# One product of ones for the exponentials of key tiles 0 and 1, summed by GpSimd, and a rewritten order of a group

## The reference, cut to what matters

```python
x = x + L0_attn(layernorm(x)); x = x + L0_ffn(layernorm(x))
x = x + L1_attn(layernorm(x)); x = x + L1_ffn(layernorm(x))
# both attentions: 2 batches x 1024 positions, 32 query heads and 8 key/value heads of 32
q, k, v = rope(x @ wq), rope(x @ wk), x @ wv
scores = einsum('bqhd,bkhd->bhqk', q, k) / sqrt(32) + causal_mask
attn = softmax(scores, axis=-1)                # exp(scores - rowmax) / sum over keys
out = einsum('bhqk,bkhd->bqhd', attn, v) @ wo
```

## Time and profile before

| | |
|---|---|
| median of 3 runs | 2916.91 us (2914.6 to 2921.62) |
| profiled execution | 2913.83 us, span of its instructions 2912.1 us |
| busy PE / DVE / ACT / POOL | 90% / 62% / 38% / 39% |
| mean granted TensorE clock | 0.952 of 2.4 GHz |
| PE in 118 to 497 us (groups of layer 0, batch 0) | 351.56 of 379 us busy |
| PE in 164 to 211 us (one of these groups) | idle 0.8 us |

### The profile page before, as it was taken

The page is one execution under the profiler, slowest core; times in us unless marked ns, Lnnn a source line. Parts: engine busy times, 40 slices in busy tenths (PEclk is TensorE's granted clock), DMA queues, the critical chain, the costliest instruction groups (busy, mean ns, idle before and its releaser), DMA issues. The chain is left out here.

```text
span 2912.1 us, 50930 instructions
## 1 busy us (share of the span) xinstructions
PE 2608.1 (90%) x15312; PEld 1828.1 (63%) x15312; DVE 1797.7 (62%) x4437; ACT 1095.2 (38%) x2381; POOL 1123.9 (39%) x801
## 2 busy tenths in 40 slices
PE   7999997999998799791969999979999987997999
PEld 6665653765654588681857565537656544876887
DVE  5677775667775433588756777765677753215543
ACT  2345454145555211470622454541354553002000
POOL 7456553546564100000054656545466642002110
PEclk9999998999999999896979999989999998998999
DMA  4323222422321421000244232213232314434111
GB/s 158 110 78 93 84 61 66 140 84 80 98 77 38 168 72 58 1 1 0 98 151 124 74 103 67 82 66 120 80 104 77 93 40 152 147 109 149 71 60 44
DMA packets 121086, 253.05 MB, mean 87 GB/s; under 512 B 12720, under 2 KB 39728, under 8 KB 120880
## 3 DMA queue, kind: packets, MB, share of 16 engines
q1 hardware_dynamic: 120912, 251.03, 27.0%
HBM read 166.57 MB, written 84.41 MB: 86 GB/s over the span
## 5 line engine op out<-in xcount | busy, mean ns | idle before, releaser
L617 ACT ACTIVATE a_prob<-a_pst 128x512 f32<-128x512 f32 (+3 forms) x1536 | 660.6, 493 | 560.4 <-PE a_pst L898 555.1
L710 DVE CUSTOM_DVE_ANT_0 a_psh<-a_psh,a_edge 128x128 f32<-128x128 f32 (+3 forms) x1024 | 479.7, 516 | 193.6 <-PE a_psh L851 172.6
L898 PE MATMUL a_pst<-a_qst,a_kst 128*128 128x512 f32 (+2 forms) x1536 | 487.9, 372 | 24.0 <-DMA a_qst<-rowmax 19.0
L851 PE MATMUL a_psh<-a_kst,a_qst 127*128 127x512 f32 (+3 forms) x1536 | 484.2, 363 | 16.2 <-DVE a_mx L710 6.1
L517 POOL TENSOR_TENSOR a_prob<-a_prob 128x2048 f32<-128x2048 f32 (+1 forms) x96 | 405.6, 4226 | 239.7 <-PE a_ppv L914 239.7
L851 PEld LDWEIGHTS a_psh<-a_kst,a_qst 127*128 127x128 f32 x1536 | 272.0, 189 | 229.8 <-DVE a_mx L713 92.7
L713 DVE TENSOR_REDUCE a_mx<-a_psh 128x1 f32<-128x512 f32 x512 | 329.1, 685 | 124.7 <-PE a_psh L851 123.7
L898 PEld LDWEIGHTS a_pst<-a_qst,a_kst 128*128 128x128 f32 x1536 | 287.5, 194 | 167.1 <-ACT a_prob L617 104.3
L914 PE MATMUL a_ppv<-a_prob,a_vg 128*32 128x512 f32 (+3 forms) x3072 | 319.8, 503 | 0.0
L502 POOL TENSOR_SCALAR_AFFINE_SELECT a_prob<-a_prob 128x512 f32<-128x512 f32 x256 | 161.8, 639 | 192.3 <-ACT a_prob L617 192.2
L927 PE MATMUL a_pden<-a_prob,a_ones 128*32 128x512 f32 (+3 forms) x2304 | 222.5, 479 | 14.1 <-POOL a_prob L517 14.1
(11 more groups left out here) (231 smaller groups left out, 4208.3 us busy)
## 6 DMA issues: line engine op xcount, KB each, us to landing
a_qst<-q SPq DMA_DIRECT2D x192, 256.0 KB, 4.5
a_wraw<-in_wqkv SPq DMA_DIRECT2D x52, 512.0 KB, 4.3
q<-a_stg_hi SPq DMA_DIRECT2D x64, 256.0 KB, 2.1
q<-a_stg_lo SPq DMA_DIRECT2D x64, 256.0 KB, 2.4
a_kst<-kT SPq DMA_DIRECT2D x96, 128.0 KB, 2.5
oT<-a_oT SPq DMA_DIRECT2D x32, 256.0 KB, 2.4
oT<-a_vT SPq DMA_DIRECT2D x32, 256.0 KB, 2.9
h_oraw<-oT SPq DMA_DIRECT2D x16, 512.0 KB, 4.0
```

The source lines that it names most:

```text
L617: act.activation(prob[k % len(prob)][:, h, off:], pst[:, (k * GH + h) % 3, off:], ACT.Exp, scale=scale).then_inc(s["exp_done"], 1)
L710: part = dve.tensor_tensor_reduce(scores, scores, edge[:, BANK - n:], 1.0, 2 * MASKED, ALU.add, ALU.max, mx_hq[kc][:, h, qt:qt + 1])
L851: mm = pe.matmul(psh[:, at, i * n:(i + 1) * n], qst[par][0:P - 1, h, qt * P:(qt + 1) * P], kst[par][0:P - 1, kc * BANK:kc * BANK + n], sta ...
L898: pe.matmul(pst[:, (k * GH + h) % 3, off:], kst[par][:, ki * P:(ki + 1) * P], qst[par][:, h, qc * BANK + off:(qc + 1) * BANK], start=True, ...
```

## The change

The new text of `ORDER`, nothing else. `SUM:0+1` and `D:0+1` take the place of `D:0` and `D:1`: POOL adds the 384 columns of each head of unit 1 onto unit 0, and one product of 512 columns per head gives the denominators of both. Around it most words of the group stand in another place.

```diff
     P:0.0 P:0.1
-    ST:0.0 WL ST:0.1 ST:0.2 S P:0.2 ST:0.3 P:0.3
-    ST:1.0 ST:1.1 P:0.4 ST:1.2 S HI:1 ST:1.3 P:0.5
-    ST:2.0 ST:2.1 P:0.6 LO:1 S P:0.7 ST:2.2 S ST:2.3
-    ST:3.0 V:0 D:0 S S ST:3.1 ST:3.2 S ST:3.3 V:1
-    ST:4.0 ST:4.1 RS:1 ST:4.2 HI:0 S S D:1 ST:4.3 LO:0
-    ST:5.0 S ST:5.1 S V:2 V:3 D:2 D:3 S ST:5.2 S ST:5.3 S V:4 S
...
-    ST:11.0 S ST:11.1 ST:11.2 P:1.0 P:1.1 ST:11.3 S P:1.2 S D:8+9 WS V:10 V:11 RK D:10 D:11 MT P:1.3
-      NORM:0 P:1.4 P:1.5 P:1.6 P:1.7 NORM:1 VG
+    ST:0.0 WL ST:0.1 ST:0.2 P:0.2 P:0.3 ST:0.3
+    ST:1.0 S ST:1.1 P:0.4 ST:1.2 S ST:1.3 HI:1 LO:1 P:0.5
+    ST:2.0 V:0 S ST:2.1 RS:1 S SUM:0+1 ST:2.2 ST:2.3 P:0.6 P:0.7
+    ST:3.0 ST:3.1 S ST:3.2 V:1 ST:3.3 S S S D:0+1
+    ST:4.0 S ST:4.1 ST:4.2 S S ST:4.3 V:2 HI:0 D:2 S
+    ST:5.0 ST:5.1 S V:3 S ST:5.2 LO:0 S ST:5.3
...
+    ST:11.0 ST:11.1 P:1.1 ST:11.2 ST:11.3 WS S S V:10 D:8+9 V:11 D:10 D:11 P:1.2 MT NORM:0 P:1.3 RK P:1.4
+      VG P:1.5 NORM:1 P:1.6 P:1.7
```

More of the change, by code:

```diff
@@ L78 @@
     P:0.0 P:0.1
-    ST:0.0 WL ST:0.1 ST:0.2 S P:0.2 ST:0.3 P:0.3
-    ST:1.0 ST:1.1 P:0.4 ST:1.2 S HI:1 ST:1.3 P:0.5
-    ST:2.0 ST:2.1 P:0.6 LO:1 S P:0.7 ST:2.2 S ST:2.3
-    ST:3.0 V:0 D:0 S S ST:3.1 ST:3.2 S ST:3.3 V:1
-    ST:4.0 ST:4.1 RS:1 ST:4.2 HI:0 S S D:1 ST:4.3 LO:0
-    ST:5.0 S ST:5.1 S V:2 V:3 D:2 D:3 S ST:5.2 S ST:5.3 S V:4 S
[L85 to L89, removed]
-    ST:11.0 S ST:11.1 ST:11.2 P:1.0 P:1.1 ST:11.3 S P:1.2 S D:8+9 WS V:10 V:11 RK D:10 D:11 MT P:1.3
-      NORM:0 P:1.4 P:1.5 P:1.6 P:1.7 NORM:1 VG
+    ST:0.0 WL ST:0.1 ST:0.2 P:0.2 P:0.3 ST:0.3
[4 more added lines that the diff above has]
+    ST:5.0 ST:5.1 S V:3 S ST:5.2 LO:0 S ST:5.3
+    ST:6.0 S D:3 V:4 S ST:6.1 ST:6.2 S ST:6.3 S
+    ST:7.0 S SUM:4+5 S ST:7.1 V:5 RS:0 V:6 ST:7.2 S ST:7.3 D:4+5
+    ST:8.0 SUM:6+7 S ST:8.1 ST:8.2 S ST:8.3 S S
+    ST:9.0 S ST:9.1 V:7 S ST:9.2 ST:9.3 S D:6+7 S S V:8 SUM:8+9 S
+    ST:10.0 S ST:10.1 S ST:10.2 V:9 S S ST:10.3 P:1.0
+    ST:11.0 ST:11.1 P:1.1 ST:11.2 ST:11.3 WS S S V:10 D:8+9 V:11 D:10 D:11 P:1.2 MT NORM:0 P:1.3 RK P:1.4
+      VG P:1.5 NORM:1 P:1.6 P:1.7
 """
```

## The result

| | before | after |
|---|---|---|
| median | 2915.97 us | 3000.52 us (2995.81 to 3003.38, 4 runs) |
| ratio to before | | 1.0285, 95% interval 1.0272 to 1.0298 |
| span of the profiled execution | 2912.1 us | 3001.7 us |
| mean granted TensorE clock | 0.952 | 0.942 |

The change makes the kernel 85 us slower; the forecast was 3000 us. In this part and the next, sums of waits are over the whole program.

What follows compares the result with a forecast made beforehand. PE, 90% busy, was taken to bound the kernel. Groups 1 to 5 add 60 us, group 6 18, group 7 6, group 0 minus 1: plus 83, forecast 3000 us; likeliest case 2965 to 3030, 8-in-10 range 2935 to 3070.

Steps and rivals of the forecast that it cites:

- two late chains: Start of a group: keys reach S:0 late, wait 0.9 us, within V:0's total 2.8 us wait for POOL's late mask.
- signs of being wrong: V:0 without a wait, clock below 1.00 inside groups 1 to 5, PE waiting at D:0+1, or groups at 47 us.
- The products: PE in each group: D:1 goes, minus 0.66 us, one more switch, plus 0.32; net minus 0.34, 11 us in 32 groups.
- one turn of 0.32: PE going over to the 32-column V and D products and back, 0.32 us; 12 per group become 13.
- Rotation behind NORM:1: Group boundary: NORM:1 waits for ACT's copies, delaying P:1's rotation; POOL's mask of unit 0 ends at 218.0 instead of 214.67.
- Keys: RK behind NORM:0's store: key loads land at plus 3.4 us, S:0 reached at 2.5 waits 0.9.
- V:0: PE reaches V:0 at plus 5.2, mask seen at 8.0: 2.8 us wait, about 1.9 shown as waiting for the mask.
- The clock, a rival with 0.12: PE's clock falls after the waits, 3 us lost each time, 72 us in all, 3071 us; chance 0.12.
- Its case for group 6: Clock slowdown would come first in group 6, where PE was forecast to wait 7.0 us for the mask.
- S:11: Late rotation delays HI:1, LO:1 and four DMAs: queries at plus 18.6, PE arrives at 17.6 and waits 1.0 us.
- D:0+1 and the sum: Sum ends at 13.3, PE reaches D:0+1 at 13.5, 0.2 us spare; group 7 loses 1.5 us, four times.
- The transpose: PE's wait before the transpose of the row maxima stays 0.56 us, since the same work precedes it in both orders.

Runs made afterwards that it cites:

- the two pairs of runs with and without the sum: Changed kernel with NORM:1 behind the rotation and RK ahead of D:10: 2949.82 us with SUM:0+1, 2942.21 without; reordered kernel with fewer product switches: 2933.24 with, 2955.95 without.
- 11 turns and no D:1: Kernel before with the sum alone: V:0 moved up before P:0.7, SUM:0+1 behind it, D:0+1 behind V:1 replacing D:0 and D:1; 2929.13 us, ratio 1.0044.
- 10 turns and no D:1: Kernel before with a new ORDER: sum kept, NORM:1 behind rotation, RK ahead of MT, V:0 and S:11 late, V and D products grouped; 2933.24 us, ratio 1.0068.
- The kernel with both taken back: Changed kernel with NORM:1 back behind P:1.7 and the rotation, and RK back ahead of D:10; sum and rest of the order stay; 2949.82 us, ratio 1.0116.
- The run with the keys late alone: Kernel before with only RK moved behind NORM:0's store; 3028.19 us, ratio 1.038.
- the reordered kernels: Kernel before with an ORDER grouping V and D products: 2933.24 us; without the sum 2955.95; last S ahead of ST:11.3 2906.16; also S:2 and S:3 later 2885.52.
- the fastest one: Kernel before with V and D products grouped, the sum, the last S ahead of ST:11.3, and S:2 and S:3 behind P:0.5; 2885.52 us, ratio 0.9896.

## Why the prediction was right

The time (3000 forecast, 3000.5 measured) and the mechanism held: two late chains, to S:0 and to V:0, and the wait at S:11 cost the time. That the number came out within 1 us is luck, since two terms were off and cancelled. The starts of ACT's copies of chunk 1 (L624) and windows between them give the loss by kind of group:

| us a group | forecast | measured |
|---|---|---|
| groups 1 to 5, 20 of them | +3.0 | +3.3 |
| of this, PE waits | +3.3 | +2.3 |
| of this, PE busy | -0.34 | +1.0 |
| group 6, 4 of them | +4.5 | +4.7 |
| group 7, 4 of them | +1.5 | +0.6 |

Over the profiled execution that is 62 us of waits and 27 us of busy time, where about 94 and minus 11 were forecast; the 3 us of 90 that the table leaves out lie in group 0 and outside the groups. Two of the prediction's own signs of being wrong were seen: V:0 without a wait (in 5 of the 20 groups), and a granted clock below 1.00 inside groups 1 to 5 (in 7 of them).

- **The products.** This is the term that was mis-sized, net minus 11 us. Minus 0.66 a group for D:1 is near: 18 us of busy time and 23 us of run time in the two pairs of runs with and without the sum. But the order was priced at one turn of 0.32, 10 us, and costs PE 24 us of busy time with the same products at the same clock. So with both chains short PE is busy 7 us more than before, not 11 less. What in the order costs the rest was not taken apart; counting turns doesn't predict it (12 turns 2608 us, 11 turns and no D:1 2603, 10 turns and no D:1 2584).
- **Rotation behind NORM:1.** Right in kind: in the boundary shown NORM:1 starts behind ACT's copies, the rotation at plus 2.7 (forecast 3.0), POOL's masks at plus 6.8 to 8.1 (forecast mask 0 done at 7.9, measured 7.5). The kernel before with this edit lost 59 us. My own test of it in the changed kernel gave 14 instead of 35 to 60, as the key loads held the same place.
- **Keys.** Forecast 0.9 us at S:0, measured 1.61 in the boundary shown and 34.5 us in all. The median landing of a key load rose from 2.5 us to 3.2; it is 3.1 or 3.2 in the three kernels that issue it right behind the 256 KB store of chunk 0, and 2.5 to 2.7 in all others. That is the mis-sized part: the keys were forecast for plus 3.4 and came at 4.2.
- **V:0.** Forecast 1.9 us a group for the mask, measured 15.4 us in 21 waits. Where PE does wait, V:0 starts at plus 7.6 to 8.0 in all groups but one, as forecast. The longer wait at S:0 takes part of it over, and where the clock falls behind that wait, slower products take the rest: in the boundary shown first, two 256-column products at 221.77 take 0.58 us instead of 0.40 and V:0's own eight 1.61 instead of 1.06. The window there:

```profile
221.00:223.00 2.00, 2.00 (x10) 1.77 (x9) 0.47 (x5) 1.27 (x3) 1.86 (x3) 0.71 0.59 227
```

- **The clock, a rival with 0.12.** It came about in part. The kernel with both taken back has the same products and as many turns; it is busy 2614.9 us at a mean clock of 0.953, the changed one 2635.5 at 0.942. That puts some 21 us on the clock, not the 72 of the rival. In the first batch it fell in two groups and not in the next two:

```profile
163.70:216.00 52.30, 48.33 (x307) 28.80 (x306) 35.77 (x97) 24.96 (x55) 31.31 (x20) 0.97 0.28 81
216.00:266.00 50.00, 48.03 (x306) 28.18 (x305) 35.29 (x96) 24.66 (x55) 31.29 (x20) 0.97 0.29 81
266.00:317.00 51.00, 46.88 (x307) 27.70 (x306) 35.60 (x97) 24.79 (x56) 31.30 (x20) 1.00 0.28 82
317.00:367.00 50.00, 46.89 (x307) 27.68 (x307) 35.46 (x97) 24.68 (x55) 31.36 (x20) 1.00 0.30 83
```

Its case for group 6 came true: the clock falls in all four of them, and there PE waits less than the 7.0 us forecast for V:0 (1.8 to 2.6 us at S:0 and 0.3 to 1.9 at V:0) and is busy 1.9 us longer. In the first, behind a wait of 2.61 us the four products of S:0 took 1.12 us, 0.66 in the boundary shown above.

```profile
421.95 1.12 PE L851 MATMUL a_psh<-a_kst,a_qst 127*128 127x128 f32 x4 [2.61 <-DMA a_kst<-kT]
```

The Trainium skill, TensorE: Matmul & The Clock Gate, Part 1, makes the clock follow how busy PE has been. The run with the keys late alone (waits of 78 us, clock 0.934, busy time plus 51) agrees with it.

- **S:11.** Forecast a wait of 1.0 us instead of some 0.25: 22.7 us in 26 waits instead of 6.1 in 10, and 19 us came back when it was moved. But I put it down to the late rotation; with the rotation on time it still waited 27.9 us. Its own earlier place in the order is enough for that wait.
- **D:0+1 and the sum.** "It just fits" held (3.2 us in all), and also that this is so only as V:0 is late: with both chains short the row is 6.2 us. In group 7 the sum was forecast to cost 6 us in all; the group lost 2.3.
- **The transpose.** Forecast unchanged at 0.56 us, measured 0.36: 15.6 us became 10.8.

## What to carry to other kernels

When PE is fed by in-order queues, follow what stands behind each moved word on every engine, down to the DMA: moving NORM ahead of a rotation and a load behind a store cost far more than the product saved. Two chains that end at the same place hide each other: taking one away moves little or nothing (14 and 0 us of 51 here), so test them together. A product saved pays only where its sum and its place in the run of PE's products are free; after that, a race of 0.04 us between two engines can be worth 27 us. And a total that comes out right proves no term: compare waits and busy time with the forecast one by one.

## What the runs showed of the hardware

- A DVE operation of 16 columns with both inputs in SBUF lasts 0.174 us alone and 2.33 us if a POOL operation of 2.35 us began 0.04 us earlier; with a start ahead of POOL's (0.27 us in the group looked at) the same instruction takes 0.176 us. The Trainium skill, SBUF — State Buffer, section SBUF: two separate sides, states this lock for a whole instruction, for whichever starts first, where the GpSimd operation reads SBUF too; the traces agree.
- Waits of 3.3 us in 24 groups cost 78 us as waits and 51 us more as PE busy time at a mean granted clock of 0.934 instead of 0.952.
- DVE stands still for 2.0 to 2.2 us behind NORM:1 twice in each batch, 8 times in the program, at both places where its loop over pairs of groups goes back to its start, with nothing that the trace shows to wait for. It does so in the kernel before too (18.3 us in nine waits of L710, which L709 is in the reordered kernels) and in the fastest one. Moving two S out of its way on PE was worth 21 us.
